# The edge products of a wavelet mix move ahead of the first analysis of a group

## The chip, the cores and the metric

The kernel runs on one core of one Trainium2 chip. The metric is device time in microseconds (us) from start to end of one execution; it is given as the median of several runs.

## The reference

For x of shape (8, 512, 207, 64), batch, time, node and channel, each (batch, node, channel) row of 512 times goes through a wavelet transform of three levels, its four components are weighted for each channel, the transform is undone, the channels are mixed by a 64x64 matrix, and x and a bias are added:

```
a = sig
for _ in range(_LEVEL):
    a, d = _dwt(a)
    details.append(d)
...
enh.append((c.reshape(-1, D, m) * w[i][None, :, None]).reshape(-1, m))
...
rec = _idwt(rec[:, :d.shape[-1]], d)
...
return x + xr @ proj_w.T + proj_b
```

## The kernel before

The transform is linear, so the kernel does it with matrices. Time is cut into 4 windows of 128, which are the partitions. Each window needs 128 coefficients of its own and 20 of its neighbour (the halo). The work is tiled in pairs of nodes (128 columns of nodes times channels); four pairs make a group (512 columns), 9 groups make a turn, and there are 23 turns, so 207 groups. The first and the last turn are written out, and a hardware loop runs over the ones between.

For each group TensorE does, all written by hand in one order (turn_of, L423):

- **analysis** of a pair (analyse, L350, matmul L364): four matmuls, x as weights and the analysis matrix moving, into coefs_ps, a single buffer that the four pairs use in turn. Before it starts it waits at L362 until VectorE has scaled the pair before. Where a pair is the first of a slot of x, it also waits for the load of that slot (L360).
- **projection** of a window (project, L381, matmul L389): four matmuls by the 64x64 matrix (two copies on the diagonal of a 128x128 one). A small projection (project_tail, L396) does the halo columns that cross the seam between the windows.
- **synthesis** of a window (synthesise, L400, matmuls L407, L408, L409): the inverse transform, in three products of a high and a low part with 512 columns each. It waits for VectorE's low part (L401) and for the addition that emptied its PSUM bank (L404).
- **edge products** (synthesise_edges, L411, matmul L418): twelve matmuls of 32 rows each, in three steps of four, which stand in the four row quarters of the array. They add the halo's share to the four windows' banks. They wait at L412 for tail_lo, which GpSimd makes (L316).

The f32 matmuls L364 and L389 show as two instructions each in the profile, so a block of four is a row of x8.

Analysis runs one group ahead, and synthesis of window 3 and the edge products run one group behind, inside the next group's order. VectorE scales the coefficients of each pair out of PSUM (scale_pair, L520), makes the low parts (split_low, L526), transposes the tail (L536) and adds the finished windows to x (add_window, L546, which waits for the edge products through `completed`). Its order in a group is written by hand too: L526 of window 0, L520 of pair 0, two L546, L526 of window 1, L520 of pair 1, two L546, L526 of window 2, L520 of pair 2, L536, L526 of window 3, L520 of pair 3. ScalarE copies the high parts (L493) and the tail's (L498). GpSimd adds the halo at the seam (L311), the bias (L323) and makes tail_lo (L316). SP loads and stores x in slots of 18 nodes.

Of the kernel before, what the change touches and what calls it, by code (L numbers as in the profile page):

```python
# [153 lines left out]
def wavelet_mix(nc, x, comp_w, w_t, bias, analysis_m, synthesis_m, edge_m, out):  # L154
# [11 lines left out]
    with ExitStack() as ctx:  # L166
# [180 lines left out]
        def _(pe):  # L347
            pe.wait_ge(analysis_loaded, 16)

            def analyse(turn, g, p, first):  # L350
                done = (turn * GROUPS + g) * PAIRS + p
                local = g * PAIRS + p
                slot = local // SLOT_PAIRS
                if first and slot == 0:
                    for i in range(3):
                        if 2 * local == FIRST_NODES[i]:
                            pe.wait_ge(first_loaded[i], 16)
                elif local % SLOT_PAIRS == 0:
                    before = 0 if slot == 0 else 16 * SLOT_DMAS
                    pe.wait_ge(loaded[slot], turn * (16 * SLOT_DMAS) + before)  # L360
                if not (first and local == 0):
                    pe.wait_ge(scaled, done)  # L362
                for w in range(WINDOWS):
                    mm = nc.tensor.matmul(coefs_ps[:, w // PART_WINDOWS, AT[w]:AT[w] + COLS],  # L364
                                          x_sb[:, w, local * PAIR:(local + 1) * PAIR],
                                          analysis_sb[:, ORDER_OF[w], :],
                                          start=w % PART_WINDOWS == 0, stop=w % PART_WINDOWS == PART_WINDOWS - 1,
                                          skip_group_check=True)
                mm.then_inc(analysed, 1)
# [11 lines left out]
            def project(turn, g, w, first):  # L381
                group = turn * GROUPS + g
                ps = wait_for_bank(turn, g, TILE_ORDER.index(w), first)
                for p in range(PAIRS):
                    if w == 0:
                        pe.wait_ge(scaled, group * PAIRS + (p + 1))
                    elif w == 2:
                        pe.wait_ge(seamed, group * PAIRS + (p + 1))
                    mm = nc.tensor.matmul(ps[:, p * PAIR:(p + 1) * PAIR], coefs_of(g, p)[:, own_cols(w)], w_sb[:, :],  # L389
                                          start=True, stop=True)  # L390
                mm.then_inc(projected, 1)

            def project_tail(turn, g, first):
                ps = wait_for_bank(turn, g, TILE_ORDER.index(TAIL), first)
                at = (g % COEF_SETS) * PAIRS
                nc.tensor.matmul(ps[:, 0:PAIRS * QUAD], w_sb[:, :],  # L396
                                 coefs_sb[:, at:at + PAIRS, PART_COLS:PART_COLS + QUAD],
                                 start=True, stop=True).then_inc(projected, 1)

            def synthesise(turn, g, w, first):  # L400
                group = turn * GROUPS + g  # L401
                pe.wait_ge(lo_copied, group * WINDOWS + (w + 1))
                if not (first and g == 0):
                    pe.wait_ge(summed, group * WINDOWS + (w + 1 - WINDOWS))  # L404
                rec = synth_ps[:, w, :]
                hi, lo = synthesis_hi[:, ORDER_OF[w], :], synthesis_lo[:, ORDER_OF[w], :]
                nc.tensor.matmul(rec, lo, proj_hi[w][:, :], start=True, stop=False)  # L407
                nc.tensor.matmul(rec, hi, proj_lo[w][:, :], start=False, stop=False)  # L408
                nc.tensor.matmul(rec, hi, proj_hi[w][:, :], start=False, stop=False).then_inc(synthesised, 1)  # L409

            def synthesise_edges(turn, g):  # L411
                pe.wait_ge(tail_lo_copied, turn * GROUPS + g + 1)  # L412
                source_hi, source_lo = proj_hi[1:] + [tail_hi], proj_lo[1:] + [tail_lo]
                for step, (weight, moving) in enumerate(((edge_lo, source_hi), (edge_hi, source_lo),
                                                         (edge_hi, source_hi))):
                    for w in range(WINDOWS):
                        rows = quad(EDGE_QUAD[w])
                        mm = nc.tensor.matmul(synth_ps[:, w, :], weight[rows, :], moving[w][rows, :],  # L418
                                              start=False, stop=step == 2)
                        if step == 2:  # L420
                            mm.then_inc(completed, 1)

            def turn_of(turn, first=False, last=False):  # L423
                for g in range(GROUPS):
                    def analyse_ahead(p):
                        if g + 1 < GROUPS:
                            analyse(turn, g + 1, p, first)
                        elif not last:
                            analyse(turn + 1, 0, p, False)

                    def synthesise_behind(w):
                        if g > 0:
                            synthesise(turn, g - 1, w, first)
                        elif not first:
                            synthesise(turn - 1, GROUPS - 1, w, False)

                    def edges_behind():
                        if g > 0:
                            synthesise_edges(turn, g - 1)
                        elif not first:  # L440
                            synthesise_edges(turn - 1, GROUPS - 1)

                    project(turn, g, 0, first)
                    synthesise_behind(3)
                    analyse_ahead(0)
                    edges_behind()
                    project(turn, g, 1, first)
                    analyse_ahead(1)
                    synthesise(turn, g, 0, first)
                    project(turn, g, 2, first)  # L450
                    analyse_ahead(2)
                    synthesise(turn, g, 1, first)
                    project_tail(turn, g, first)
                    project(turn, g, 3, first)
                    analyse_ahead(3)
                    synthesise(turn, g, 2, first)
# [3 lines left out]
            pe.wait_ge(w_loaded, 2 * 16)  # L460
            pe.wait_ge(lo_built, 2)
            turn_of(0, first=True)
            with nc.Fori(1, TURNS - 1, engines=(ENG.PE,), hint_back_edge=True) as turn:
                turn_of(turn)
            turn_of(TURNS - 1, last=True)
            synthesise(TURNS - 1, GROUPS - 1, 3, False)
            synthesise_edges(TURNS - 1, GROUPS - 1)
# [144 lines left out]
```

## Time and profile before

| | us |
|---|---|
| median of 3 runs | 2462.91 (2462.81 to 2463.53) |
| the profiled execution | 2463.63 |
| its span | 2461.8 |
| TensorE matmul busy | 2433.9 (99%) |
| TensorE weight load busy | 2203.3 (89%) |
| VectorE busy | 1896.4 (77%) |
| ScalarE busy | 626.5 (25%) |
| GpSimd busy | 1473.9 (60%) |

The span is the time from the first to the last instruction of the program; the execution's own time also holds what lies around it. A busy time is the union of an engine's instructions. Matmuls are pipelined and their ends are modelled, so the starts of matmuls tell more than their durations. A group in the timeline is one or more equal instructions: its start, its length from first start to last end, and their number.

### The profile page before, as it was taken

What the parts mean: (1) busy time and instruction counts of PE and PEld (TensorE: products, weight loads), DVE (VectorE), ACT (ScalarE), POOL (GpSimd) and SP (SyncE); (2) the same over time, 40 slices, a digit from 0 to 9 for tenths busy, and PEclk for the clock granted to TensorE, in tenths of its full rate; (3) what the DMA queues carried; (4) which work ended last, traced back from release to release, by engine and by line L of the source; (5) the groups of instructions that cost most, each with busy time, mean ns of one, the idle gap of its engine ahead of it and who ended that gap; (6) DMA issues with size and microseconds to landing.
All of it is one profiled execution on the core that took longest, in us unless ns stands there. A gap on an engine that the chain in (4) does not pass through costs nothing.

```text
span 2461.8 us, 51862 instructions
## 1 busy us (share of the span) xinstructions
PE 2433.9 (99%) x18630; PEld 2203.3 (89%) x18630; DVE 1896.4 (77%) x3315; ACT 626.5 (25%) x1038; POOL 1473.9 (60%) x1908
## 2 busy tenths in 40 slices
PE   7999999999999999999999999999999999999998
PEld 7999999999999999999999999999999989998987
DVE  4777777777777777777777777777777777777776
ACT  1222222222222222222222222222222222222222
POOL 4656665666656666665666666566665665666555
PEclk9999999999999999999999999999999999999999
DMA  3544454454544544454454544544454454644543
GB/s 129 200 174 179 173 197 153 168 216 153 222 162 153 204 173 177 171 195 153 172 211 153 227 157 153 208 174 177 170 192 157 172 207 153 230 154 153 212 162 128
DMA packets 106160, 435.35 MB, mean 177 GB/s; under 512 B 6288, under 2 KB 7696, under 8 KB 106128
## 3 DMA queue, kind: packets, MB, share of 16 engines
q1 hardware_dynamic: 105232, 434.13, 46.7%
q10 hardware_dynamic: 896, 0.79, 0.1%
q8 instruction: 20, 0.33, 0.1%
q14 instruction: 12, 0.10, 0.0%
HBM read 217.84 MB, written 217.06 MB: 177 GB/s over the span
## 4 chain that ended last, share of the span: by engine, by line
PE 98%; POOL 0%; issue 0%; DVE 0%; DMA 0%; ACT 0%; ACTq 0%; DVEq 0%; POOLq 0%
PE coefs_ps L364 34%; PE proj_ps L389 32%; PE synth_ps L409 8%; PE synth_ps L408 8%; PE synth_ps L407 8%; PE synth_ps L418 8%; PE proj_ps L396 2%; DMA comp_sb<-comp_w 0%; POOL scale_sb L301 0%; POOL tail_lo L316 0%; DVE x_sb L546 0%; DVE coefs_sb L520 0%; DVE proj_lo L526 0%; ACT proj_hi L493 0%; ACTq L166 0%
## 5 line engine op out<-in xcount | busy, mean ns | idle before, releaser
L323 POOL TENSOR_TENSOR x_sb<-x_sb,bias_sb 128x512 f32<-128x512 f32 x828 | 1052.7, 1271 | 5.2 <-issue 5.2
L364 PE MATMUL coefs_ps<-analysis_sb,x_sb 128*128 128x148 f32 x6624 | 975.3, 290 | 12.7 <-DMA analysis_sb<-analysis_m 9.1
L493 ACT ACTIVATE proj_hi<-proj_ps 128x512 fp32r<-128x512 f32 x828 | 494.6, 597 | 1807.1 <-PE proj_ps L389 1807.1
L389 PEld LDWEIGHTS proj_ps<-w_sb,coefs_sb 128*128 128x128 f32 x6624 | 835.3, 192 | 118.1 <-issue 82.8
L364 PEld LDWEIGHTS coefs_ps<-analysis_sb,x_sb 128*128 128x128 f32 x6624 | 895.6, 191 | 32.3 <-DMA analysis_sb<-analysis_m 9.1
L389 PE MATMUL proj_ps<-w_sb,coefs_sb 128*128 128x128 f32 x6624 | 897.5, 278 | 2.3 <-issue 1.6
L526 DVE TENSOR_TENSOR proj_lo<-proj_ps,proj_hi 128x512 fp32r<-128x512 f32 x828 | 573.0, 692 | 422.7 <-ACT proj_hi L493 408.9
L311 POOL TENSOR_TENSOR coefs_sb<-coefs_sb 128x20 f32<-128x20 f32 x828 | 187.2, 226 | 810.1 <-DVE coefs_sb L520 778.8
L520 DVE TENSOR_TENSOR coefs_sb<-coefs_ps,scale_sb 128x552 f32<-128x552 f32 x828 | 600.6, 725 | 86.8 <-PE coefs_ps L364 75.2
L546 DVE TENSOR_TENSOR x_sb<-synth_ps,x_sb 128x512 f32<-128x512 f32 x828 | 531.5, 684 | 32.4 <-PE synth_ps L418 29.7
L407 PE MATMUL synth_ps<-proj_hi,synthesis_lo 128*128 128x512 f32 x828 | 404.0, 488 | 0.7 <-DVE proj_lo L526 0.7
L316 POOL TENSOR_TENSOR tail_lo<-tail_sb,tail_hi 32x512 fp32r<-32x512 f32 x207 | 262.0, 1266 | 154.5 <-ACT tail_hi L498 151.3
L409 PE MATMUL synth_ps<-proj_hi,synthesis_hi 128*128 128x512 f32 x828 | 326.9, 395 | 0.0
L408 PE MATMUL synth_ps<-proj_lo,synthesis_hi 128*128 128x512 f32 x828 | 326.3, 394 | 0.0
L536 DVE STREAM_TRANSPOSE tail_sb<-proj_ps 32x128 f32<-32x128 f32 x828 | 259.6, 313 | 14.9
L409 PEld LDWEIGHTS synth_ps<-proj_hi,synthesis_hi 128*128 128x128 f32 x828 | 155.5, 188 | 35.6
L407 PEld LDWEIGHTS synth_ps<-proj_hi,synthesis_lo 128*128 128x128 f32 x828 | 157.7, 190 | 1.1 <-DVE proj_lo L526 1.1
L408 PEld LDWEIGHTS synth_ps<-proj_lo,synthesis_hi 128*128 128x128 f32 x828 | 157.7, 191 | 0.0
L498 ACT ACTIVATE tail_hi<-tail_sb 32x512 fp32r<-32x512 f32 x207 | 129.9, 628 | 5.2
L418 PE MATMUL synth_ps<-proj_hi,edge_lo 32*128 32x512 f32 x621 | 104.2, 497 | 1.3 <-POOL tail_lo L316 1.3
L418 PE MATMUL synth_ps<-tail_hi,edge_lo 32*128 32x512 f32 x207 | 102.7, 496 | 0.0
L396 PEld LDWEIGHTS proj_ps<-coefs_sb,w_sb 128*128 128x128 f32 x414 | 77.9, 188 | 19.1
(22 smaller groups left out, 644.5 us busy)
## 6 DMA issues: line engine op xcount, KB each, us to landing
out<-x_sb SPq DMA_DIRECT2D x184, 1152.0 KB, 6.0
x_sb<-x SPq DMA_DIRECT2D x182, 1152.0 KB, 11.2
x_sb<-x SPq DMA_DIRECT2D x1, 1024.0 KB, 9.6
x_sb<-x SPq DMA_DIRECT2D x1, 768.0 KB, 6.0
x_sb<-x SPq DMA_DIRECT2D x1, 512.0 KB, 4.2
bias_sb<-bias ACTq DMA_DIRECT2D x1, 256.0 KB, 6.9
analysis_sb<-analysis_m ACTq DMA_DIRECT2D x1, 222.0 KB, 7.0
synthesis_sb<-synthesis_m ACTq DMA_DIRECT2D x1, 192.0 KB, 6.9
```

Source lines behind the costliest of these rows:

```text
L316: nc.gpsimd.tensor_tensor(tail_lo[tail_rows, :], tail_sb[tail_rows, :], tail_hi[tail_rows, :].bitcast(fp32), ALU.subtract).then_inc(tail_l ...
L323: nc.gpsimd.tensor_tensor(cols, cols, bias_sb[:, :], ALU.add).then_inc(biased, 1)
L364: mm = nc.tensor.matmul(coefs_ps[:, w // PART_WINDOWS, AT[w]:AT[w] + COLS], x_sb[:, w, local * PAIR:(local + 1) * PAIR], analysis_sb[:, OR ...
L389: mm = nc.tensor.matmul(ps[:, p * PAIR:(p + 1) * PAIR], coefs_of(g, p)[:, own_cols(w)], w_sb[:, :], start=True, stop=True)
L407: nc.tensor.matmul(rec, lo, proj_hi[w][:, :], start=True, stop=False)
L408: nc.tensor.matmul(rec, hi, proj_lo[w][:, :], start=False, stop=False)
L409: nc.tensor.matmul(rec, hi, proj_hi[w][:, :], start=False, stop=False).then_inc(synthesised, 1)
L418: mm = nc.tensor.matmul(synth_ps[:, w, :], weight[rows, :], moving[w][rows, :], start=False, stop=step == 2)
L493: nc.scalar.activation(proj_hi[w][:, :], proj_ps[BANK[g][TILE_ORDER.index(w)]][:, :], ACT.Copy).then_inc(hi_copied, 1)
L520: nc.vector.tensor_tensor(coefs_of(g, p).rearrange("c (two k) -> c two k", two=PARTS)[:, :, 0:PART_COLS], coefs_ps[:, :, 0:PART_COLS], sca ...
L526: nc.vector.tensor_tensor(proj_lo[w][:, :], proj_ps[BANK[g][TILE_ORDER.index(w)]][:, :], proj_hi[w][:, :].bitcast(fp32), ALU.subtract).the ...
L546: nc.vector.tensor_tensor(cols, synth_ps[:, w, :], cols, ALU.add).then_inc(summed, 1)
```

## The change

In each group the call for the edge products of the group before moves from behind to ahead of the analysis of the next group's pair 0. It then follows straight on the synthesis of window 3.

```diff
                     project(turn, g, 0, first)
                     synthesise_behind(3)
+                    edges_behind()
                     analyse_ahead(0)
-                    edges_behind()
                     project(turn, g, 1, first)
                     analyse_ahead(1)
                     synthesise(turn, g, 0, first)
```

TensorE's queue before, around that place in the first turn's second group (weight loads are not shown; 128x148 is the analysis, 128x128 the projection; the edge products are listed with their PSUM columns):

```order
L409 MATMUL synth_ps<-proj_hi,synthesis_hi 128x512
L364 MATMUL coefs_ps<-analysis_sb,x_sb 128x148 x4
L418 MATMUL synth_ps<-proj_hi,edge_lo 128x512 x3
L418 MATMUL synth_ps<-tail_hi,edge_lo 128x512
L418 MATMUL synth_ps<-proj_lo,edge_hi 128x512 x3
L418 MATMUL synth_ps<-tail_lo,edge_hi 128x512
L418 MATMUL synth_ps<-proj_hi,edge_hi 128x512 x3
L418 MATMUL synth_ps<-tail_hi,edge_hi 128x512
L389 MATMUL proj_ps<-w_sb,coefs_sb 128x128 x4
L364 MATMUL coefs_ps<-analysis_sb,x_sb 128x148 x4
```

Between the two analyses stand the twelve edge matmuls and the projection of window 1. The same place with the change:

```order
L409 MATMUL synth_ps<-proj_hi,synthesis_hi 128x512
L418 MATMUL synth_ps<-proj_hi,edge_lo 128x512 x3
L418 MATMUL synth_ps<-tail_hi,edge_lo 128x512
L418 MATMUL synth_ps<-proj_lo,edge_hi 128x512 x3
L418 MATMUL synth_ps<-tail_lo,edge_hi 128x512
L418 MATMUL synth_ps<-proj_hi,edge_hi 128x512 x3
L418 MATMUL synth_ps<-tail_hi,edge_hi 128x512
L364 MATMUL coefs_ps<-analysis_sb,x_sb 128x148 x4
L389 MATMUL proj_ps<-w_sb,coefs_sb 128x128 x4
L364 MATMUL coefs_ps<-analysis_sb,x_sb 128x148 x4
```

The edge matmuls now stand ahead of both analyses, and between the analyses only the projection of window 1 is left. The order on the other engines is the same as before.

## Rows read from the trace of the kernel before

**Rows 1.** The page: TensorE's busy time, its granted clock, and the last chain by engine.

```profile
PE 2433.9 (99%) x18630; PEld 2203.3 (89%) x18630; DVE 1896.4 (77%) x3315; ACT 626.5 (25%) x1038; POOL 1473.9 (60%) x1908
...
PEclk9999999999999999999999999999999999999999
...
PE 98%; POOL 0%; issue 0%; DVE 0%; DMA 0%; ACT 0%; ACTq 0%; DVEq 0%; POOLq 0%
```

**Rows 2.** Waits of the whole run: us in total, times, longest us.

```profile
DVE coefs_sb L520 <- PE coefs_ps L364: 75.2, 209, 2.5
...
PE coefs_ps L364 <- DVE coefs_sb L520: 3.7, 3, 1.9
```

**Rows 3.** Timeline of matmuls at the edited joint: start us, length us, what.

```profile
1009.70 0.39 PE L409 MATMUL synth_ps<-proj_hi,synthesis_hi 128*128 128x512 f32 x1
1009.93 1.17 PE L364 MATMUL coefs_ps<-analysis_sb,x_sb 128*128 128x148 f32 x8
1011.03 0.50 PE L418 MATMUL synth_ps<-proj_hi,edge_lo 32*128 32x512 f32 x3
...
1011.60 0.39 PE L418 MATMUL synth_ps<-proj_hi,edge_hi 32*128 32x512 f32 x3
...
1011.93 1.16 PE L389 MATMUL proj_ps<-w_sb,coefs_sb 128*128 128x128 f32 x8
1012.93 0.29 PE L364 MATMUL coefs_ps<-analysis_sb,x_sb 128*128 128x148 f32 x1
```

**Rows 4.** Timeline of matmuls away from the edges, in the group before.

```profile
1001.23 1.17 PE L364 MATMUL coefs_ps<-analysis_sb,x_sb 128*128 128x148 f32 x8
...
1002.93 1.05 PE L389 MATMUL proj_ps<-w_sb,coefs_sb 128*128 128x128 f32 x8
1003.82 1.17 PE L364 MATMUL coefs_ps<-analysis_sb,x_sb 128*128 128x148 f32 x8
1004.73 0.49 PE L407 MATMUL synth_ps<-proj_hi,synthesis_lo 128*128 128x512 f32 x1
```

**Rows 5.** Timeline of matmuls in the last group, which has no analysis ahead.

```profile
2441.06 0.40 PE L409 MATMUL synth_ps<-proj_hi,synthesis_hi 128*128 128x512 f32 x1
2441.39 0.50 PE L418 MATMUL synth_ps<-proj_hi,edge_lo 32*128 32x512 f32 x3
```

**Rows 6.** Last analysis matmul of pair 0, its scaling, the next analysis's weight load.

```profile
1010.81 0.29 PE L364 MATMUL coefs_ps<-analysis_sb,x_sb 128*128 128x148 f32 x1
...
1011.13 0.73 DVE L520 TENSOR_TENSOR coefs_sb<-coefs_ps,scale_sb 128x552 f32<-128x552 f32 x1 [0.31 <-PE coefs_ps L364]
...
1012.82 0.19 PEld L364 LDWEIGHTS coefs_ps<-analysis_sb,x_sb 128*128 128x128 f32 x1
```

**Rows 7.** Prologue: scalings and the weight loads that waited for them.

```profile
12.54 0.73 DVE L520 TENSOR_TENSOR coefs_sb<-coefs_ps,scale_sb 128x552 f32<-128x552 f32 x1 [11.55 <-POOL scale_sb L301]
...
13.33 0.50 PEld L364 LDWEIGHTS coefs_ps<-analysis_sb,x_sb 128*128 128x128 f32 x2 [2.27 <-DVE coefs_sb L520]
...
18.94 0.73 DVE L520 TENSOR_TENSOR coefs_sb<-coefs_ps,scale_sb 128x552 f32<-128x552 f32 x1 [2.49 <-PE coefs_ps L364]
19.73 0.29 PEld L364 LDWEIGHTS coefs_ps<-analysis_sb,x_sb 128*128 128x128 f32 x1 [1.19 <-DVE coefs_sb L520]
```

**Rows 8.** Timeline of VectorE from the low part of window 1 on.

```profile
1013.75 0.69 DVE L526 TENSOR_TENSOR proj_lo<-proj_ps,proj_hi 128x512 fp32r<-128x512 f32 x1 [0.44 <-ACT proj_hi L493]
1014.36 0.72 DVE L520 TENSOR_TENSOR coefs_sb<-coefs_ps,scale_sb 128x552 f32<-128x552 f32 x1
1015.00 1.28 DVE L546 TENSOR_TENSOR x_sb<-synth_ps,x_sb 128x512 f32<-128x512 f32 x2
```

**Rows 9.** Timeline of GpSimd: the tail's low part for the edges at 1011.03.

```profile
1008.23 1.26 POOL L316 TENSOR_TENSOR tail_lo<-tail_sb,tail_hi 32x512 fp32r<-32x512 f32 x1 [0.72 <-ACT tail_hi L498]
```

**Rows 10.** A weight load and the matmul in flight beside it, in synthesis 3.

```profile
1009.14 0.48 PE L407 MATMUL synth_ps<-proj_hi,synthesis_lo 128*128 128x512 f32 x1
...
1009.23 0.19 PEld L408 LDWEIGHTS synth_ps<-proj_lo,synthesis_hi 128*128 128x128 f32 x1
```

## The prediction

> **What bounds the kernel now.** I read the page first: TensorE matmuls are busy 99% of the span, the clock is granted in full in every slice, and the chain that ended last is 98% TensorE [rows 1]. So the time is the length of TensorE's own queue plus whatever holds it up. Next the list of waits: in the whole run TensorE's analysis matmuls stood still for VectorE's scaling (L520) 3 times, 3.7 us in all, while VectorE stood still for the analyses 209 times [rows 2]. Those few are in the prologue. The scaling is slow enough to matter, but something covers it. Last the timeline, a stretch at a time, since the order of short blocks is all that changes. I count in starts, because the ends of matmuls overlap the next ones.
>
> At the joint that is edited, the queue goes L409 (last matmul of synthesis 3), analysis of pair 0, edge products, projection 1, analysis of pair 1. From the L409 at 1009.70 to the analysis of pair 1 at 1012.93 is **3.23 us** [rows 3]. Entering and leaving the edge products costs something beside their own work: an analysis takes 0.91 us to the next full-width block (1003.82 to 1004.73), but 1.10 us to the edges (1009.93 to 1011.03); the projection behind the edges takes 1.00 us to the next block (1011.93 to 1012.93), but 0.89 us elsewhere (1002.93 to 1003.82) [rows 3, 4]. The 0.11 us of the latter is a weight load that could not be made ahead.
>
> **The change, part by part.** Nothing is added or removed: per group one block of 12 edge matmuls goes ahead of one block of analysis matmuls. There are 207 groups; the first has no edges behind it and the last has no analysis ahead, so the order differs in 205. In the last group of before, edges already stand straight behind synthesis 3, which prices that joint.
>
> *1. TensorE's own work, with no wait counted.* New order: L409 to edges 0.33 us (2441.06 to 2441.39) [rows 5]; edges to what follows 0.90 us (1011.03 to 1011.93) [rows 3]; then the analysis of pair 0. Its seven steps take 0.88 us (1009.93 to 1010.81) [rows 3, 6] and an eighth 0.13, and I add the 0.11 of the bare weight load: 1.12 us. Then projection 1, now inside full-width work, 0.89 us [rows 4]. Sum: 0.33 + 0.90 + 1.12 + 0.89 = **3.24 us** against 3.23. So the edges cost the same wherever they stand: nothing, 0.01 x 205 = 2 us at most.
> The one joint that the trace lacks is edges to analysis. Its bounds: from below free, with both the 0.11 and the drain saved (edges to next 0.90, of which L418 at 1011.60 to the next block is 0.33, against 0.23 from L409 to the analysis) [rows 3], together 0.20 us; from above the 0.20 that the exit to a projection costs, and a tenth more. I take 0.20, since the analysis starts with a weight load of the same shape as the projection does.
> The Trainium skill (TensorEngine Tiling (Array Packing), Key Properties) says that a change of tiling mode drains the engine; by that rule both drains are still paid, one on entry and one on exit, and the sum stays at 3.24. The entries of the trace agree, behind an analysis and behind a synthesis.
>
> *2. The wait that appears.* coefs_ps is one buffer: the analysis of pair 1 (L362) waits until VectorE has scaled pair 0. Before, edges and projection 1 stood between: scaling ran from 1011.13 for 0.73 us, to 1011.86, and the weight load of pair 1 came at 1012.82, 0.96 us later [rows 6]. After, projection 1 stands there alone. From L409 of synthesis 3 as zero:
> - last matmul of the analysis of pair 0: 0.33 + 0.90 + 0.11 + 0.88 = 2.22;
> - scaling starts 0.32 later (1010.81 to 1011.13) [rows 6], at 2.54, takes 0.73, ends 3.27. VectorE is free: it did L526 of window 0 before, whose input is not later than now;
> - the weight load comes about 0.06 us after the scaling ends. In the prologue, where nothing covers this, the scaling at 12.54 takes 0.73 and the load comes at 13.33; the same at 18.94 and 19.73 [rows 7]. So the load is at 3.33;
> - it is bare, as behind the edges: another 0.11, so the matmul does useful work from 3.44.
>
> Without the wait it would from 3.24. The period grows by 3.44 - 3.23 = **0.21 us**, of which 0.20 is the new stall. Times 205: 43 us. Once per turn pair 1 opens a slot of x and waits for that load too (L360), which takes one more instruction of the queue; I allow 0.06 us for it, as long as one hand-over, x 23 = 1.4 us. Bounds for it: nothing and twice that.
>
> *3. Behind the stall.* Queued behind the held analysis are synthesis 0, projection 2 and the rest, all shifted alike. On VectorE, the two additions L546 no longer wait for edges, so they follow the scaling directly: start at 2.54 + 0.64 = 3.18, the next 0.60 later (two of 0.68 take 1.28 together), and after another 0.60 L526 of window 1 at 4.38, the scaling of pair 1 at 4.99 (0.61 later), end 5.71, load possible at 5.77 [rows 8]. TensorE wants that load (pair 2) at 3.44 + 2.59 - 0.11 = 5.92, since analysis to analysis is 2.59 us (1001.23 to 1003.82) [rows 4]. Slack 0.15 us, and it is there only because the first stall moved pair 2 back. ScalarE's copy of window 1 let L526 start at 1013.75, 4.05 behind L409 [rows 8]; the new 4.38 is later, so the copy holds nothing.
>
> *4. The wait on the tail (L412).* The edges now want tail_lo 0.33 us behind L409, at 1010.03 in the old numbers. GpSimd starts it at 1008.23, for 1.26, to 1009.49 [rows 9]: 0.54 us in hand, so it costs nothing. Were that cover gone, each us of lateness would be a us per period. Edges done earlier help additions and copies off the path only.
>
> Sum: the profiled execution took 2463.6 us (span 2461.8); plus 43, plus 1.4, is 2508. The median of the runs is 0.7 us under the profiled one, so the forecast is **2507 us**.
>
> **The rivals.**
> *Late, but not bare.* The held weight load costs only its lateness: 3.33 against 3.23, 0.10 x 205 + 1.4 = 22 us, 2485 us. That would be so if the load in front of pair 1 were never hidden anyway. The Trainium skill (TensorE: Matmul & The Clock Gate, Part 3, The mechanism) says that a weight load overlaps matmuls in flight only if its row group differs, by which the exposure is already paid at every full-width block. The rows speak against it: the load of L408 starts at 1009.23 while L407, of the same 128 rows, runs from 1009.14 for 0.48 us [rows 10]. Chance 0.06.
> *A second wait at pair 2.* VectorE's chain of five operations is my estimate from separate joints, with 0.15 us to spare. If it comes out 0.25 or more longer, pair 2 stalls too, by 0.1 and its load by up to 0.11: 20 to 43 us more, 2527 to 2550. For it: two additions now press on the scaling. Chance 0.08.
> *No difference.* The exit from the edges is free before an analysis: all up to pair 0's end comes 0.20 earlier, and the load of pair 1 is at 3.13, the work at 3.24: 2464 to 2467. Chance 0.04.
> *Faster.* TensorE fetches the analysis weights, which depend on nothing but x, ahead of what holds the matmul, at both places: the exit is free and the load of pair 1 is hidden. Then pair 1 works from 3.13, 0.10 us earlier, 2443 us. It decides where pair 0's last matmul comes before 2.12. Against it: in the prologue the load itself waited for the scaling, not only the matmul [rows 7], and at the exit the load stands with the matmul. Chance 0.04.
>
> **How the numbers follow.** Forecast 0.78, rivals 0.06, 0.08, 0.04, 0.04. A measurement can tell about 0.2% (5 us) from no change. Slower: forecast and the first two rivals, 0.92, taken as 0.90 for what I have not seen; same 0.05, faster 0.05. Range: 2484 takes in the late load; above, 2507 plus 0.1 us per period for the drain, the chain of VectorE and rounding of a dozen rows is 2528. The rest is left out.
>
> **What would show it.** L409 to edges 0.33; edges to analysis 0.33 behind the last step; analysis of pair 0 to projection 1 about 1.12; projection 1 to pair 1's load 1.0 or more with an idle gap released by L520, about 200 times, and none at pair 2; scaling of pair 0 to that load 0.06; period 11.92 instead of 11.71; clock in full. It is wrong if no gap appears in front of pair 1, if the first gap behind that load is 0.13 and not 0.23, or if L418 waits for L316.

## The result and the profile after

The changed kernel takes **2509.61 us** (median of 4 runs, 2508.53 to 2509.69) against 2463.22 us for the kernel before on the same chip: a ratio of 1.0188, 95% interval 1.0168 to 1.0208, or 46.4 us more. One of the four runs of the kernel before took 3507.81 us and its reason is not known; the other three have a median of 2462.91, 46.7 us under the changed kernel. The forecast was 2507 in a range of 2484 to 2528.

The page of the changed kernel, the lines that answer to [rows 1]:

```profile
PE 2478.1 (99%) x18630; PEld 2194.4 (88%) x18630; DVE 1848.1 (74%) x3315; ACT 626.8 (25%) x1038; POOL 1477.9 (59%) x1908
...
PEclk9999999999999999999999999999999999999999
...
PE 98%; issue 0%; DVE 0%; POOL 0%; DMA 0%; ACTq 0%; ACT 0%; DVEq 0%; POOLq 0%
```

A reader of the page alone would find nothing: TensorE is as busy as before, and the clock is as high. The stall is shorter than the modelled tail of the matmul in front of it, so the matmuls' busy time hides it. The list of waits of the changed kernel says a little more (us in total, times, longest):

```profile
DVE coefs_sb L520 <- PE coefs_ps L364: 303.9, 209, 4.0
...
PEld coefs_ps L364 <- DVE coefs_sb L520: 12.5, 44, 2.0
```

VectorE now stands idle 303.9 us ahead of its scalings where it was 75.2 in [rows 2], because the edges now stand ahead of the analysis whose result it waits for, and no additions fill that time. And the weight loads of analyses waited for the scaling 44 times. The list leaves out the shortest idle gaps, so the other stalls, of 0.12 us of visible gap, are not in it. The timeline shows them all. Matmuls of the changed kernel at the edited joint, a group in the middle of a turn:

```profile
1122.97 0.40 PE L409 MATMUL synth_ps<-proj_hi,synthesis_hi 128*128 128x512 f32 x1
1123.30 0.50 PE L418 MATMUL synth_ps<-proj_hi,edge_lo 32*128 32x512 f32 x3
...
1123.87 0.40 PE L418 MATMUL synth_ps<-proj_hi,edge_hi 32*128 32x512 f32 x3
...
1124.21 1.27 PE L364 MATMUL coefs_ps<-analysis_sb,x_sb 128*128 128x148 f32 x8
1125.32 1.05 PE L389 MATMUL proj_ps<-w_sb,coefs_sb 128*128 128x128 f32 x8
1126.30 0.52 PE L364 MATMUL coefs_ps<-analysis_sb,x_sb 128*128 128x148 f32 x2
...
1127.32 0.49 PE L407 MATMUL synth_ps<-proj_hi,synthesis_lo 128*128 128x512 f32 x1
```

Every joint is within 0.01 us of its forecast: L409 to edges 0.33, edges to analysis 0.91, analysis to projection 1.11, then 0.98 to pair 1's analysis where [rows 4] has 0.89, and that analysis takes 1.02 (1126.30 to 1127.32) where it took 0.91. From L409 to pair 1 it is 3.33 us, against 3.23 in [rows 3], and 0.10 more follows inside pair 1. The period of a group is 11.91 us (11.92 was forecast) where it was 11.71. The hand-over at the same place, in the timelines of TensorE's matmuls, VectorE and the weight loads:

```profile
1125.19 0.29 PE L364 MATMUL coefs_ps<-analysis_sb,x_sb 128*128 128x148 f32 x1
...
1125.52 0.73 DVE L520 TENSOR_TENSOR coefs_sb<-coefs_ps,scale_sb 128x552 f32<-128x552 f32 x1 [1.41 <-PE coefs_ps L364]
1126.17 1.28 DVE L546 TENSOR_TENSOR x_sb<-synth_ps,x_sb 128x512 f32<-128x512 f32 x2
1127.36 0.68 DVE L526 TENSOR_TENSOR proj_lo<-proj_ps,proj_hi 128x512 fp32r<-128x512 f32 x1
1127.96 0.72 DVE L520 TENSOR_TENSOR coefs_sb<-coefs_ps,scale_sb 128x552 f32<-128x552 f32 x1
...
1126.30 0.19 PEld L364 LDWEIGHTS coefs_ps<-analysis_sb,x_sb 128*128 128x128 f32 x1
...
1128.88 0.30 PEld L364 LDWEIGHTS coefs_ps<-analysis_sb,x_sb 128*128 128x128 f32 x2
```

Pair 0's last matmul is at 1125.19, the scaling ends at 1126.25, the load follows at 1126.30. This replaces the 0.96 us in hand of [rows 6]. The scaling of pair 1 ends at 1128.68 and the load of pair 2 comes at 1128.88, 0.20 later: no stall there, with 0.15 in hand over the hand-over of 0.05.

In two of the nine groups of a turn the stall is 0.10 longer. The same three in the second group of a turn:

```profile
1101.27 0.29 PE L364 MATMUL coefs_ps<-analysis_sb,x_sb 128*128 128x148 f32 x1
...
1101.69 0.73 DVE L520 TENSOR_TENSOR coefs_sb<-coefs_ps,scale_sb 128x552 f32<-128x552 f32 x1 [1.50 <-PE coefs_ps L364]
...
1102.48 0.19 PEld L364 LDWEIGHTS coefs_ps<-analysis_sb,x_sb 128*128 128x128 f32 x1 [0.22 <-DVE coefs_sb L520]
```

The scaling starts 0.42 us behind the last matmul instead of 0.33. In these groups VectorE's queue does a register operation for the second wait (L519), from 1101.60 to 1101.65, only after the first wait is over; in the others that wait is dealt with about 1.6 us ahead of the last matmul. There are two such groups for each of the 21 turns of the loop, 42 in all, and they make up all but two of the 44 listed waits. Together: 0.20 x 205 = 41 us, and 0.10 x 42 = 4.1 us.

The rest of 1 us comes from the first and the last turn, and its largest part from one place of the last; other stalls there are a little shorter than before. GpSimd stands there once for 3.1 us with no releaser, in both kernels, right ahead of the tail's low part for which the edge products wait. From the lists of waits, the kernel before and then the changed one:

```profile
POOL tail_lo L316 <- issue: 3.2, 1, 3.2
PE synth_ps L418 <- POOL tail_lo L316: 1.3, 2, 0.9
...
POOL tail_lo L316 <- issue: 3.1, 1, 3.1
PE synth_ps L418 <- POOL tail_lo L316: 2.2, 2, 1.9
```

The edges stand earlier in the new order, so they have less cover: the start of the edges comes 1.9 us late here, where it was 1.0. Behind this wait TensorE's granted clock is 0.56 for 2 us (2428.80 to 2430.80), and the whole group is 3.4 us longer than its neighbours, against 1.0 before.

### The profile page after: what moved, and what is told of

Its sections match the earlier page's. It is cut to its first block, busy times and chain, and to the rows that moved or that the text cites. A ratio compares the mean times of both kernels' runs of the same rounds, so it can differ in the third digit from the quotient of the medians.

```text
span 2507.9 us, 51862 instructions
## 1 busy us (share of the span) xinstructions
PE 2478.1 (99%) x18630; PEld 2194.4 (88%) x18630; DVE 1848.1 (74%) x3315; ACT 626.8 (25%) x1038; POOL 1477.9 (59%) x1908
## 4 chain that ended last, share of the span: by engine, by line
PE 98%; issue 0%; DVE 0%; POOL 0%; DMA 0%; ACTq 0%; ACT 0%; DVEq 0%; POOLq 0%
PE coefs_ps L364 37%; PE proj_ps L389 29%; PE synth_ps L409 8%; PE synth_ps L407 8%; PE synth_ps L408 8%; PE synth_ps L418 7%; PE proj_ps L396 2%; DMA comp_sb<-comp_w 0%; POOL scale_sb L301 0%; DVE x_sb L546 0%; DVE coefs_sb L520 0%; POOL tail_lo L316 0%; DVE proj_lo L526 0%; ACTq L166 0%; DVEq L166 0%
## 5 line engine op out<-in xcount | busy, mean ns | idle before, releaser
L364 PE MATMUL coefs_ps<-analysis_sb,x_sb 128*128 128x148 f32 x6624 | 1018.8, 297 | 14.0 <-DMA analysis_sb<-analysis_m 9.2
L364 PEld LDWEIGHTS coefs_ps<-analysis_sb,x_sb 128*128 128x128 f32 x6624 | 879.4, 191 | 118.3 <-issue 76.4
L389 PE MATMUL proj_ps<-w_sb,coefs_sb 128*128 128x128 f32 x6624 | 876.2, 275 | 2.5 <-issue 1.6
L520 DVE TENSOR_TENSOR coefs_sb<-coefs_ps,scale_sb 128x552 f32<-128x552 f32 x828 | 599.6, 724 | 315.4 <-PE coefs_ps L364 303.9
L316 POOL TENSOR_TENSOR tail_lo<-tail_sb,tail_hi 32x512 fp32r<-32x512 f32 x207 | 262.0, 1266 | 153.3 <-ACT tail_hi L498 150.2
L409 PE MATMUL synth_ps<-proj_hi,synthesis_hi 128*128 128x512 f32 x828 | 326.7, 395 | 0.0
L409 PEld LDWEIGHTS synth_ps<-proj_hi,synthesis_hi 128*128 128x128 f32 x828 | 155.4, 188 | 35.9
L418 PEld LDWEIGHTS synth_ps<-proj_hi,edge_lo 32*128 32x128 f32 x621 | 39.0, 182 | 78.2 <-issue 75.1
L418 PE MATMUL synth_ps<-proj_hi,edge_lo 32*128 32x512 f32 x621 | 104.1, 497 | 2.2 <-POOL tail_lo L316 2.2
L418 PE MATMUL synth_ps<-tail_hi,edge_lo 32*128 32x512 f32 x207 | 103.4, 499 | 0.0
```

Of the source, the lines that this page charges most:

```text
L316: nc.gpsimd.tensor_tensor(tail_lo[tail_rows, :], tail_sb[tail_rows, :], tail_hi[tail_rows, :].bitcast(fp32), ALU.subtract).then_inc(tail_l ...
L520: nc.vector.tensor_tensor(coefs_of(g, p).rearrange("c (two k) -> c two k", two=PARTS)[:, :, 0:PART_COLS], coefs_ps[:, :, 0:PART_COLS], sca ...
```

## The experiments

The edits are given against the changed kernel or the kernel before, as each says. In the kernels with added lines, the line numbers in the rows are one to five higher than in the text.

**e1: the scaling cut at the PSUM bank, in the changed kernel.**

```diff
-                nc.vector.tensor_tensor(coefs_of(g, p).rearrange("c (two k) -> c two k", two=PARTS)[:, :, 0:PART_COLS],
-                                        coefs_ps[:, :, 0:PART_COLS], scale_sb[:, :, :],
-                                        ALU.mult).then_inc(scaled, 1)
+                for part, done in enumerate((scaled_first, scaled)):
+                    nc.vector.tensor_tensor(coefs_of(g, p)[:, part * PART_COLS:(part + 1) * PART_COLS],
+                                            coefs_ps[:, part, 0:PART_COLS], scale_sb[:, part, :],
+                                            ALU.mult).then_inc(done, 1)
...
-                if not (first and local == 0):
-                    pe.wait_ge(scaled, done)
                 for w in range(WINDOWS):
+                    if w % PART_WINDOWS == 0 and not (first and local == 0):
+                        pe.wait_ge(scaled_first if w == 0 else scaled, done)
```

> The change, with the scaling of each pair cut at the PSUM bank: two operations of 276 columns, each with its own count, and the analysis waits for the first bank before its first matmul and for the second bank before its third. Nothing is left out. Theory (the loss is the analysis of pair 1 waiting for the scaling of pair 0): the first half ends about 0.33 + 0.45 = 0.78 us behind pair 0's last matmul, the load can follow at 0.83 and is wanted at 0.905, so the wait goes and the time falls to 2465 us; groups 0 and 1 of a turn, whose scaling starts 0.10 later, may still lose 0.13 each, 44 times, so 2464 to 2471. Rival (the edges cost more where they now stand, next to the synthesis and ahead of an analysis): the time stays within 5 us of 2509.

It took 2515.27 us (ratio 1.0212, interval 1.0198 to 1.0226): by the time alone the theory is refuted, and the rival is nearer, though a little more than its 5 us away. The trace says otherwise. The load of pair 1 and the joint behind it, in the timelines of loads and matmuls:

```profile
1127.30 0.19 PEld L365 LDWEIGHTS coefs_ps<-analysis_sb,x_sb 128*128 128x128 f32 x1
...
1134.56 1.25 PE L390 MATMUL proj_ps<-w_sb,coefs_sb 128*128 128x128 f32 x8
1135.57 0.48 PE L408 MATMUL synth_ps<-proj_hi,synthesis_lo 128*128 128x512 f32 x1
...
1135.32 0.19 PEld L390 LDWEIGHTS proj_ps<-w_sb,coefs_sb 128*128 128x128 f32 x1
```

Pair 0's last matmul was at 1126.40 (its scaling starts 0.33 later, at 1126.72, below); the load of pair 1 is 0.90 behind it, just as wanted, so the stall at pair 1 is gone. A new one of 0.20 stands in projection 0 of the next group: it takes 1.01 us (1134.56 to 1135.57) where it took 0.80 to 0.81. Its load for pair 3 comes at 1135.32. VectorE in the same stretch:

```profile
1126.72 0.80 DVE L522 TENSOR_TENSOR coefs_sb<-coefs_ps,scale_sb 128x276 f32<-128x276 f32 x2 [1.40 <-PE coefs_ps L365]
1127.44 1.28 DVE L548 TENSOR_TENSOR x_sb<-synth_ps,x_sb 128x512 f32<-128x512 f32 x2
1128.63 0.68 DVE L528 TENSOR_TENSOR proj_lo<-proj_ps,proj_hi 128x512 fp32r<-128x512 f32 x1
...
1133.87 0.69 DVE L528 TENSOR_TENSOR proj_lo<-proj_ps,proj_hi 128x512 fp32r<-128x512 f32 x1
1134.48 0.79 DVE L522 TENSOR_TENSOR coefs_sb<-coefs_ps,scale_sb 128x276 f32<-128x276 f32 x2
```

From the scaling of pair 0 to that of pair 3, which ends at 1135.27, it has no listed idle time at all. Projection 0 waits for that end, 0.05 before its load. So this kernel meets a second bound straight behind the first: VectorE's chain within a group. The additions of windows 0 and 1 are part of it, and they stand behind the scaling of pair 0.

The cut itself has a share in this bound. Two halves take 0.72 us from their start to that of the next operation (1126.72 to 1127.44), where the whole took 0.65 (1125.52 to 1126.17 in the changed kernel). Over the four scalings of the chain this is 0.28 us, more than the new stall of 0.20. So, by this estimate, the chain of whole scalings would have ended about 0.08 us ahead of what projection 0 wants: the second bound is shown for the new order with the cut, and not for the change by itself.

**e3: the same cut in the kernel before.**

> The kernel before, with the same cut of the scaling as in e1_bank_split. Theory: the scaling is covered there with 0.9 us in hand, so the time stays at 2463 within 2 us, which shows that the cut itself gives and costs nothing; e1_bank_split less this one is what the place of the edges costs with no wait, 0.01 us per group or 2 us at most. Rival (the cut makes VectorE's chain shorter and that was worth something everywhere): 2455 or less.

2465.11 us (ratio 1.0009, interval 1.0000 to 1.0019). The cut costs some 2 us and gives nothing where the order of before leaves room: VectorE still has idle time in its chain there.

**e4: half the scaling of pair 0 once more, in the changed kernel; e5: the same in the kernel before.**

```diff
+                if p == 0:
+                    nc.vector.tensor_tensor(coefs_of(g, p)[:, 0:PART_COLS], coefs_ps[:, 0, 0:PART_COLS],
+                                            scale_sb[:, 0, :], ALU.mult).then_inc(half_scaled, 1)
+                    dve.wait_ge(half_scaled, group + 1)
```

> The change, with VectorE's first half of the scaling of pair 0 done once more ahead of the whole one (same result; the second waits for the first), so the scaling ends later by 0.45 us for 276 columns and about 0.1 to 0.2 for the hand-over. Theory: the analysis of pair 1 waits for it fully exposed, so each group grows by just that, 0.55 to 0.65 us x 206 = 113 to 134 us: 2622 to 2644. Rival (the stall is something else and VectorE has room): 2509 to 2520.

> The kernel before, with the same half scaling once more in pair 0. Theory: the scaling of pair 0 has 0.90 us in hand behind the edges and projection 1, more than the 0.55 to 0.65 that is added; the two additions then start about 0.3 us later and still end before the copy of window 1 lets the next operation start. So nothing: 2463 within 3 us. Rival (VectorE's chain is tight before the change too): 2480 or more.

e4 took 2613.12 us, 103.5 more than the changed kernel. Its timeline:

```profile
1170.26 0.45 DVE L522 TENSOR_TENSOR coefs_sb<-coefs_ps,scale_sb 128x276 f32<-128x276 f32 x1 [1.41 <-PE coefs_ps L365]
1170.74 0.73 DVE L525 TENSOR_TENSOR coefs_sb<-coefs_ps,scale_sb 128x552 f32<-128x552 f32 x1
...
1171.53 0.19 PEld L365 LDWEIGHTS coefs_ps<-analysis_sb,x_sb 128*128 128x128 f32 x1 [0.60 <-DVE coefs_sb L525]
```

The whole scaling starts 0.48 later (I had guessed 0.55 to 0.65, with a hand-over that turned out to be 0.03), and 0.48 x 206 = 99 us: all of it appears in the time. In the trace the way from projection 1 to pair 1 grows by 0.48 us in every group. The 4.6 us that are left are one stall of the last turn, where VectorE stood 3.6 us with no releaser ahead of a scaling, and that group is 5 us longer. In e5 the same 0.48 gives 7 us in all (2470.36, ratio 1.0027, interval 1.0017 to 1.0038), not the nothing within 3 that I expected. In its loop the groups are as long as before; the 7 us fall in one place of the last turn, as its list of waits for the last 169 us shows:

```profile
DVE coefs_sb L525 <- issue: 4.7, 1, 4.7
PEld coefs_ps L365 <- DVE coefs_sb L525: 4.2, 1, 4.2
```

Once, VectorE stood 4.7 us for nothing that the profile names, right in front of a scaling, and TensorE waited 4.2 us with it. The other 2.8 us are TensorE's clock, which was granted at 0.50 for the 5.3 us behind this wait (the lower of its two levels, 1.2 GHz). A projection there:

```profile
2405.12 1.91 PE L390 MATMUL proj_ps<-w_sb,coefs_sb 128*128 128x128 f32 x8
```

The same eight matmuls take 1.05 us at full clock [rows 4]. The group is 6.9 us longer than its neighbours, which is the whole difference. So the scaling of pair 0 does have 0.48 us of room in the order of before.

**e2: the two waits in front of the scaling in the other order, in the changed kernel.**

```diff
-                dve.wait_ge(analysed, group * PAIRS + (p + 1))
                 if p == 0 and not (first and g < COEF_SETS):
                     dve.wait_ge(projected, (group - COEF_SETS + 1) * TILES)
+                dve.wait_ge(analysed, group * PAIRS + (p + 1))
```

> The change, with the two waits in front of the scaling of pair 0 in the other order, the long-fulfilled one (projected) first. In groups 0 and 1 of a turn the profile of the change shows a register operation of 46 ns behind the wait for the analysis, and the scaling starts 0.42 us behind the last matmul instead of 0.33. Theory: that start falls to 0.33 in all groups and 44 x 0.097 = 4.3 us go: 2505 us. Rival (the two groups are late for another reason, such as the load of x): no difference, 2509.

2511.00 us (1.0194, interval 1.0180 to 1.0208): no gain. In the loop the effect is there. In the second group of a turn, matmul and scaling:

```profile
1100.15 0.29 PE L364 MATMUL coefs_ps<-analysis_sb,x_sb 128*128 128x148 f32 x1
...
1100.48 0.73 DVE L520 TENSOR_TENSOR coefs_sb<-coefs_ps,scale_sb 128x552 f32<-128x552 f32 x1 [1.41 <-PE coefs_ps L364]
```

The distance is 0.33 again. But the kernel met one stall like that of e5, at the start of the last turn, on VectorE:

```profile
2385.14 0.69 DVE L526 TENSOR_TENSOR proj_lo<-proj_ps,proj_hi 128x512 fp32r<-128x512 f32 x1 [1.35 <-ACT proj_hi L493]
2390.65 0.73 DVE L520 TENSOR_TENSOR coefs_sb<-coefs_ps,scale_sb 128x552 f32<-128x552 f32 x1 [4.82 <-issue]
```

So 4.1 us went out in 42 places and 5.0 came in at one: TensorE's wait, and behind it again a stretch at the lower clock (0.58 granted on average from 2391.90 to 2396.00). In the two turns that are written out, the new order of the waits does harm: there the scaling starts 0.40 us behind the matmul instead of 0.33, in 14 groups, 1 us in all. By time alone the run is inconclusive; by place it confirms the cause of the 0.10 in the loop.

**e6: the edges one block later, in the kernel before; e7: the same with the cut.**

```diff
                     analyse_ahead(0)
-                    edges_behind()
                     project(turn, g, 1, first)
+                    edges_behind()
                     analyse_ahead(1)
```

> The edges the other way: one block later than before, between projection 1 and the analysis of pair 1. Between the analyses of pairs 0 and 1 stands the same work as before, so pair 1 doesn't wait. But the two additions start about 0.9 us later, and behind them the low part of window 1 and the scaling of pair 1, which would end at 4.63 us behind pair 0's last matmul; the load of pair 2 could follow at 4.69 and is wanted at 4.60. Theory: a stall at pair 2 of 0.09 us and 0.11 for its bare load, 0.2 us x 205 = 41 us: 2504, range 2485 to 2520. Rival (only the cover between pairs 0 and 1 matters, or only the edges' place next to the synthesis): 2463 to 2466.

> As e6_edges_later, with the scaling cut at the bank as in e1_bank_split. Theory: the first half of pair 1's scaling ends about 0.28 us earlier than the whole did, so pair 2 finds its first bank free and the stall goes: 2463 to 2467. Rival: the time of e6_edges_later.

e6 took 2479.43 us (ratio 1.0063, interval 1.0049 to 1.0077), under the range that I had given. Its timeline, VectorE and the load of pair 2:

```profile
1114.16 1.29 DVE L546 TENSOR_TENSOR x_sb<-synth_ps,x_sb 128x512 f32<-128x512 f32 x2 [1.04 <-PE synth_ps L418]
1115.37 0.68 DVE L526 TENSOR_TENSOR proj_lo<-proj_ps,proj_hi 128x512 fp32r<-128x512 f32 x1
1115.97 0.72 DVE L520 TENSOR_TENSOR coefs_sb<-coefs_ps,scale_sb 128x552 f32<-128x552 f32 x1
...
1116.74 0.19 PEld L364 LDWEIGHTS coefs_ps<-analysis_sb,x_sb 128*128 128x128 f32 x1
```

Pair 0's last matmul was at 1112.06 (0.33 ahead of its scaling), so the load is at 4.68, forecast 4.69: the stall is at pair 2 as said. But I had added 0.11 for the bare load to its lateness of 0.09. That counts one thing twice: a load that is ahead of its matmul by 0.11 and comes 0.09 late delays the matmul by 0.09, no more. 16.0 us over 205 groups is 0.08. With that, the theory is right in place and size, and my expectation wrong by its arithmetic.

e7 took 2503.21 us (ratio 1.0162, interval 1.0148 to 1.0176), where both theory and rival had it at or under e6. In its trace pair 2 is free (its analysis takes 0.91 us again, where e6 has 1.00), and projection 0 takes 1.00 us instead of 0.81: the cut freed pair 2, and VectorE's longer chain met the second bound found in e1.

**e8: the two additions ahead of the scaling of pair 0, in the changed kernel; e9: that with the cut; e10: the cut, with projection 0 waiting for first halves only; e11: all of these with the wait order of e2.**

```diff
                     split_low(turn, g, 0)
-                    scale_ahead(0)
                     add_behind(0)
                     add_behind(1)
+                    scale_ahead(0)
```

```diff
                     if w == 0:
-                        pe.wait_ge(scaled, group * PAIRS + (p + 1))
+                        pe.wait_ge(scaled_first, group * PAIRS + (p + 1))
```

> The change, with VectorE's two additions of windows 0 and 1 ahead of the scaling of pair 0 (they can start 0.43 us behind the last edge step, so at -0.87 us against pair 0's last matmul, and end just as the scaling may start, 0.33). The whole scaling stays in one piece. Theory of two bounds: the first, pair 1 waiting for the scaling of pair 0, is untouched, so 2509, range 2506 to 2513, though VectorE's chain behind the scaling is now 1.2 us shorter. Rival (VectorE's chain as a whole is what holds the group): it falls by most of the loss, 2465 to 2485.

> As e8_adds_ahead, with the scaling cut at the bank as in e1_bank_split. Theory of two bounds: e1_bank_split took away the first and ran into the second, VectorE's unbroken chain from the scaling of pair 0 to that of pair 3, for which projection 0 waits; here both have room, so the time is that of the kernel before with the same cut (2465): 2464 to 2471, with 0.02 to 0.1 us in groups 0 and 1 of a turn. Rival (the cut itself, or the edges' place, costs what e1_bank_split lost): 2500 to 2515.

> As e1_bank_split, additions where they were; but projection 0, which reads columns of the first bank alone, waits for the first half of each scaling instead of the whole. The half of pair 3 is ready at 8.52 + 0.05 = 8.58 us behind pair 0's last matmul, and wanted at about 8.60. Theory of two bounds: the 0.2 us that e1_bank_split waited at projection 0 goes; what stays is 0.04 us at projection 3, which waits for the low part of window 2, and more in groups 0 and 1 of a turn: 2474, range 2466 to 2482. Rival: 2500 to 2515.

> The change with all four together: scaling cut at the bank, additions ahead, projection 0 waiting for first halves, and the fulfilled wait ahead of the other in front of the scaling. It is the most room that the new order can be given. Theory: TensorE's own queue is as long in both orders (3.24 against 3.23 us at the joint), so it comes to the time of the kernel before and not under it: 2463 to 2468. Rival (the new place of the edges is cheaper once nothing waits): 2455 or less.

| kernel | median us | ratio to before | 95% interval |
|---|---|---|---|
| changed | 2509.61 | 1.0188 | 1.0168 to 1.0208 |
| e1, first bound away | 2515.27 | 1.0212 | 1.0198 to 1.0226 |
| e8, second bound away | 2509.76 | 1.0190 | 1.0176 to 1.0204 |
| e9, both away | 2468.13 | 1.0020 | 1.0011 to 1.0029 |
| e10, both away another way | 2481.20 | 1.0073 | 1.0060 to 1.0087 |
| e11, all | 2466.03 | 1.0013 | 1.0004 to 1.0022 |
| e3, before with the cut | 2465.11 | 1.0009 | 1.0000 to 1.0019 |

Either cure alone gives nothing, and both together give 41.5 us (2509.61 to 2468.13). That is what two bounds of nearly the same height look like: with the first the period of a group is 11.91 us, with the second 11.93, with neither 11.73. VectorE in e9:

```profile
1104.87 1.29 DVE L548 TENSOR_TENSOR x_sb<-synth_ps,x_sb 128x512 f32<-128x512 f32 x2 [0.20 <-PE synth_ps L419]
1106.08 0.80 DVE L522 TENSOR_TENSOR coefs_sb<-coefs_ps,scale_sb 128x276 f32<-128x276 f32 x2
1107.60 0.69 DVE L528 TENSOR_TENSOR proj_lo<-proj_ps,proj_hi 128x512 fp32r<-128x512 f32 x1 [0.72 <-ACT proj_hi L494]
```

The additions fill the time in which VectorE used to wait for pair 0, and behind the scaling it now has 0.72 us idle, where in e1 it had none. e10 keeps the longer chain, and keeps the stall of 0.03 at projection 3 that was forecast; one group of each turn is another 0.3 us longer. Its time lies at the top of its range, and 4.6 us over the execution whose trace was kept, so a part of it has no trace. e11 is 2.8 us over the kernel before and 0.9 over e3, which shares the cut. No version of the new order came out under the kernel before.

## Why the prediction was right

*TensorE's own work, 3.24 against 3.23.* Right, by sum and by joint. The one joint without a row, edges to analysis, cost what it costs to a projection (1123.87 to 1124.21, 0.34, then 1.11 to the next block). e11 against e3, 2466.0 against 2465.1, is the same statement in whole kernels, and so are their periods, 11.71 and 11.72 us against 11.71 before: with nothing waiting, the place of the edges costs no more than can be told.

*The wait for the scaling.* Right. The load was forecast at 3.33 us behind L409 and is at 1126.30 - 1122.97 = 3.33. e4 shows that it is this scaling that is waited for, 0.48 us for 0.48, and e1 that the stall at pair 1 goes when the first half of it is enough. The stall is 0.20 us by lateness of the load, as the sum had it; writing it as "bare, another 0.11" was one of two ways to the same number. Of the signs that were named, the list of waits shows 44 gaps and not about 200, because most are too short for it, and the way from projection 1 to the load is 0.98, which is what the sum gives, and not "1.0 or more".

*The extra wait for a slot of x, 1.4 us.* Wrong in kind. Pair 1 of the third group of a turn, which has it, is not later than the others: the fulfilled wait is passed while the queue stands anyway. The extra that exists is VectorE's, 0.10 us in two other groups of each turn of the loop, 4.1 us. It was in the trace of before, at the same two groups, hidden behind 0.96 us of cover. I had read one group and multiplied. The forecast was short by 2.6 us. This term is 4.1 in and 1.4 out; the stall measured 0.20 and not 0.21 us, 2 us less over 205 groups; the first and the last turn added 1 us; and the median lies 0.1 us under the profiled execution and not 0.7. That the misses nearly cancel is luck.

*The wait on the tail.* Put at nothing, and right in the loop. But one of the signs of being wrong, that L418 waits for L316, does show once in the last turn, and costs 0.9 us more there than before, and 1.4 behind it with the clock granted in part. It is the wait that the prediction named, with the cover gone. The list of waits of the kernel before has GpSimd's stand; [rows 2] and [rows 9] don't.

*Behind the stall.* The slack of 0.15 us at pair 2 was right, and so was the statement that the first stall makes it. But step 3 followed VectorE's chain only as far as pair 1's scaling. Followed to pair 3 it would have shown how little room the whole chain has, by the estimate under e1 0.08 us once the first stall is gone. That changed nothing in this time, and was the first thing that I met when I took the first bound away with a cut that costs 0.28.

*The rivals.* "Late, but not bare" compared the load's time with the matmul's, the slip that e6 exposed; it needs a load that stands with its matmul even when nothing is waited for, and [rows 6] and [rows 3] have it at 1012.82, 0.11 ahead of the matmul at 1012.93. The rule of the Trainium skill that stood beside it (TensorE: Matmul & The Clock Gate, Part 3, The mechanism) is not borne out in the change's trace either: the load of pair 2 at 1128.88 stands beside the matmuls of the projection, of the same 128 rows, and where nothing waits, blocks follow at 0.89 and 0.91 us. "A second wait at pair 2" did not come in the change, and did in e6. "No difference" and "Faster" fall with the joint at 0.34 and with the load, which waited itself.

## What to carry to other kernels

When a block is moved on the engine that bounds, its own length hardly matters; ask what it stood between. A producer and its consumer on one buffer need so much other work between them (here 0.33 + 0.73 + 0.05 = 1.1 us behind the last matmul), and a block moved out from between them is cover taken away. And before curing such a wait, follow the other engine's chain through the whole period, with the cost of the cure in it: here the cut's own 0.28 us on VectorE was more than the room there, so that each cure alone was worth nothing.

## What the runs showed of the hardware beside this

- Going into the 32-row products costs 0.20 us and coming out of them another 0.20, whichever full-width block stands beside them. Going in: 1.10 us from an analysis to the edges [rows 3] where it is 0.91 to a synthesis [rows 4]; behind a synthesis 0.33 [rows 5] where it is 0.23 to an analysis [rows 3], and 0.34 instead of 0.23 between the first two steps of the edges. Coming out: 0.33 or 0.34 instead of 0.23 from the last step to a projection or an analysis, and 0.10 more inside that block, whose first weight load stands with its first matmul (both at 1124.21 in the changed kernel).
- In the loop VectorE passes a fulfilled wait whose value is computed by a register operation at no cost if it stands ahead of an open wait, and pays about 0.10 us for it if it stands behind (0.42 against 0.33 us from matmul to scaling; e2 turned one into the other). In the turns that are written out it is the other way round: 0.33 us with the fulfilled wait behind, 0.40 with it ahead.
- In the straight-line code of the last turn an engine stands now and then for some us with no releaser in the profile: VectorE once for 3.6 to 4.8 us ahead of a scaling in e2, e4 and e5, and GpSimd once for about 3 us in every kernel. Where TensorE waited for VectorE's, it cost 5 to 7 us of the whole time, a part of it by the lower clock behind it. Each of these stands ends 1.5 to 1.8 us behind the start of a packet of 8192 bytes on the DMA queue that the profile calls instruction (in e5 the packet starts at 2399.12 and VectorE goes on at 2400.91). So it may be that the engine waits for its instructions; no run tried it. Differences of that size between kernels of different code should be looked up by place before they are believed.
